# Second self attention of a decoder: scores as three products of rounded halves, and two slots for projection weights

## The chip, the cores and the metric

One core of a Trainium2 chip runs the whole program. The metric is device time in microseconds (us), the median of the runs, lower is better. The engines that matter here are TensorE (PE in the rows, its weight loads PEld), VectorE (DVE), ScalarE (ACT), GpSimd (POOL) and SyncE (SP), which issues the transfers.

## The reference, cut to what matters

The program is a decoder of two layers (self attention, cross attention, feed forward, each followed by a layer norm). The change lies in the second layer's self attention: 4 batches of 512 tokens, width 512, 16 query heads of 128, 4 key and value heads, rotary embedding, causal mask.

```python
xqkv = x @ Wqkv
xq = apply_rotary_emb(xq)                  # [b, 512, 16, 128]
xk = apply_rotary_emb(xk)                  # [b, 512, 4, 128]
xk = jnp.repeat(xk, g, axis=2)             # g = 4
xv = jnp.repeat(xv, g, axis=2)
scores = jnp.einsum('bqhd,bkhd->bhqk', xq, xk) * scale + causal_add[None, None]
probs = jax.nn.softmax(scores, axis=-1)
attn = jnp.einsum('bhqk,bkhd->bqhd', probs, xv).reshape(B, S, q_size)
x = _layernorm(x + attn @ Wo, axis=-1)
```

## The kernel before

`self_attention_1` handles one batch after another: three in a loop (`Fori`), the fourth written out behind it. In a batch, TensorE first does the pieces of `FIRST`: keys 0 and 1, a tile of values, key 2, a tile of values, key 3, query 0. Then it goes through `plan`, an order of 72 steps. Step 4h+j makes the scores of head h for the 128 query rows of tile j. A tile has only the keys that the causal mask leaves, so its scores are 128, 256, 384 or 512 columns wide. Ahead of the scores of every fourth step (j = 0) stands the projection of the NEXT head's query, `("query", h+1)`. Four steps after its scores a tile of probabilities is transposed ("turn", L109), and at step 4h+1 the values product of head h-2 follows (L1832). The products with `Wo` ("out", L1849) come in four rounds: 4 tiles of 8 heads at step 39, 4 tiles of 4 heads from step 58, 4 tiles of 2 heads from step 65, and 4 tiles of 2 heads at step 71.

Projections (L1785), value tiles (L1798) and the out products take their operands as two rounded halves, high and low (type `F32R`), and sum three products: high by high, high by low, low by high. Scores (L1820) and values products (L1832) are plain float32 matmuls; each shows in the trace as two records, that is "x2" for one score tile.

A projected query goes into one of two PSUM banks, `mm`. The other engines work in the order of their own programs, and each instruction waits for semaphores:

- VectorE applies the rotary embedding in `rotate`: three multiplications with the tables (L1922) from the bank, a drain, one addition (L1928) into `q_cols` or `k_cols`, which also frees the bank. For query h+1, which is projected in step 4h, it does so at its own step 4h+2 (`QUERY_LAG = 2`), ahead of that step's mask. In each step it adds the mask to the diagonal block (L1977), finds the row maximum (L1979) and takes the reciprocal of the sum of the step before (L1984). It also makes the low half of the attention output (L1942).
- ScalarE, in each step: the high half of the attention output where there is one (L1869), the copy of the transposed probabilities out of PSUM (L1877), the exponential of this step's scores (L1885), and the multiplication of the last step's probabilities by the reciprocal (L1891).
- GpSimd has only the end of the layer norm to do in a batch.
- SyncE loads the weights. `load_projection(p)` (L1714) brings the high and low halves of projection p (0 to 3 the keys, 4 to 19 the queries, 512 KB each) into slot p modulo `WEIGHT_SLOTS`; ahead of it SyncE waits until the projection that held the slot is done. At the start of the stage it issues key 0, the tables, key 1, the values weight (2 MB), then projections 2 and 3, then the halves of `Wo` (4 MB in three transfers, L1719), and only then does it wait for the first slot.

The lines that order TensorE at a head's first tile:

```python
elif kind == "scores":
    h, j = divmod(n, NT)
    if j == 0:
        pe.wait_ge(s.mm.free, b * MM + s.mm.size + mm_at["query", h] + 1)
    pe.wait_ge(s.sc.free, b * SC + NT + n + 1)
```

Of the kernel before, what the change touches and what calls it, by code (L numbers as in the profile page):

```python
# [27 lines left out]
P = 128  # L28
# [1597 lines left out]
def self_attention_1(nc, m, tables_in, packed):  # L1626
# [8 lines left out]
    TURN_LAG, VALUES_LAG, OUT_LAG = 4, 6, 8  # L1635
    QUERY_LAG = 2
    SLOTS = 5
    WEIGHT_SLOTS = 4
    PROJECTIONS = KV_HEADS1 + HEADS1


# [32 lines left out]
    with ExitStack() as ctx:  # L1674
# [2 lines left out]
        wo = sb("wo", [P, HALF_HEADS, 2, D], F32R)  # L1677
        tables, mask = sb("tables", [P, 2, S]), sb("mask", [P, P])
        x_high, x_low = sb("x_high", [P, KD, S], F32R), sb("x_low", [P, KD, S], F32R)
        k_cols, v_rows, q_cols = sb("k_cols", [P, KV_HEADS1, S]), sb("v_rows", [P, NT, KV_HEADS1 * HD1]), sb("q_cols", [P, 2, S])  # L1680
        turned_part = sb("turned_part", [P, S])
        neg_max, row_sum, inv_sum = sb("neg_max", [P, TILES]), sb("row_sum", [P, TILES]), sb("inv_sum", [P, TILES])
        probs = sb("probs", [P, SLOTS, S])
        x_rows = probs[:, 0:NT, :]
# [3 lines left out]
        s = Names()  # L1688
        s.x_loaded, s.max_ready, s.inv_ready, s.probs_ready, s.made = (sem(n) for n in ("x_loaded", "max_ready", "inv_ready", "probs_ready", "made"))
        s.var_ready, s.rstd_ready = sem("var_ready"), sem("rstd_ready")  # L1690
        s.x_high_ready, s.att_high_ready, s.shift_made = sem("x_high_ready"), sem("att_high_ready"), sem("shift_made")
        s.weights_in, s.wo_in = [sem(f"weights_in_{i}") for i in range(WEIGHT_SLOTS)], [sem(f"wo_in_{i}") for i in range(len(OUTS) - 1)]
        w_v, tables_loaded = sem("w_v"), sem("tables_loaded")
# [4 lines left out]
        def batches(engine, turn_x, batch):  # L1698

            turn_x(0)  # L1700
            with engine.Fori(0, B - 1) as b:
                batch(b, False)
            batch(B - 1, True)

        def bank_of(p):

# [53 lines left out]
        def _(pe):  # L1760
# [13 lines left out]
            def batch(b, last_one):  # L1774
# [33 lines left out]
                for step in plan:  # L1808
                    for kind, n in step:
                        if kind == "query":  # L1810
                            project(KV_HEADS1 + n)
                        elif kind == "v":
                            tile_values(n)
                        elif kind == "scores":
                            h, j = divmod(n, NT)
                            if j == 0:
                                pe.wait_ge(s.mm.free, b * MM + s.mm.size + mm_at["query", h] + 1)
                            pe.wait_ge(s.sc.free, b * SC + NT + n + 1)
                            t = (j + 1) * P
                            pe.matmul(sc[n % 4][:, 0:t], q_cols[:, h % 2, j * P:t], k_cols[:, h // GROUP, 0:t],  # L1820
                                      start=True, stop=True).then_inc(s.sc.full, 1)
                        elif kind == "turn":
                            pe.wait_ge(s.probs_ready, b * TILES + n + 1)
                            pe.wait_ge(s.ta.free, b * TA + n + 1)
                            turn_tile(pe, ta[n % 2], probs[:, n % SLOTS, :], m.ident[:], n % NT + 1).then_inc(s.ta.full, 1)
                        elif kind == "values":
                            g = mm_at[kind, n]
                            kv = n // GROUP
                            pe.wait_ge(s.ta.free, b * TA + s.ta.size + (n + 1) * NT)
                            pe.wait_ge(s.mm.free, b * MM + g + 1)  # L1830
                            for c in range(NT):
                                last = pe.matmul(mm[g % 2][:, c * P:], v_rows[:, c, kv * HD1:(kv + 1) * HD1],  # L1832
                                                 probs_t[:, n % 2, c, c * P:], start=c == 0, stop=c == NT - 1)
                            last.then_inc(s.mm.full, 1)
                        elif kind == "x" and not last_one:
                            turn_x(b + 1)
                        elif kind == "out":
                            o, j = divmod(n, NT)
                            first, end = OUTS[o]
                            if j == 0:  # L1840
                                for part in (range(3) if o == 0 else (o - 1,)):
                                    pe.wait_ge(s.wo_in[part], b * 32 + (16 if o == 0 else 32))
                            g = mm_at[kind, n]
# [12 lines left out]
        def _(act):  # L1856
# [4 lines left out]
                    act.copy(x_high[:, :, j * P:(j + 1) * P], blocks_of(sc[j], KD)).then_inc(s.x_high_ready, 1)  # L1861

            def batch(b, last_one):
                for now, step in enumerate(plan):
                    for kind, n in plan[now - 1] if now else ():
                        if kind == "values":
                            g = mm_at[kind, n]
                            act.wait_ge(s.mm.full, b * MM + g + 1)
                            act.copy(att_high[:, n % HALF_HEADS, :], mm[g % 2]).then_inc(s.att_high_ready, 1)  # L1869
# [33 lines left out]
        def _(dve):  # L1903
# [8 lines left out]
            def batch(b, last_one):  # L1912
# [1 line left out]
                dve.wait_ge(s.made, 2)  # L1914
                cos, sin = tables[:, 0, :], tables[:, 1, :]

                def rotate(to, g, scale):

                    dve.wait_ge(s.mm.full, b * MM + g + 1)
                    half = P // 2  # L1920
                    def times(to, rows, table):
                        dve.scalar_tensor_tensor(to, mm[g % 2][rows, :], scale, table, ALU.mult, ALU.mult)  # L1922

                    times(to, slice(0, P), cos)
                    times(turned_part[0:half, :], slice(half, P), sin[half:P, :])
                    times(turned_part[half:P, :], slice(0, half), sin[0:half, :])
                    dve.drain()
                    dve.tensor_tensor(to, to, turned_part[:], ALU.add).then_inc(s.mm.free, 1)  # L1928

                def deferred(kind, n):  # L1930
                    if kind == "x":
                        if not last_one:
                            low_x(b + 1)
                        return
                    g = mm_at[kind, n]
                    if kind == "query":
                        dve.drain()
                        rotate(q_cols[:, n % 2, :], g, 1.0)
                    elif kind == "values":
                        dve.wait_ge(s.mm.full, b * MM + g + 1)  # L1940
                        dve.wait_ge(s.att_high_ready, b * HEADS1 + n + 1)
                        dve.tensor_tensor(att_low[:, n % HALF_HEADS, :], mm[g % 2], att_high[:, n % HALF_HEADS, :].bitcast(F32),  # L1942
                                          ALU.subtract).then_inc(s.mm.free, 1)
                    elif kind == "v":
                        dve.wait_ge(s.mm.full, b * MM + g + 1)
                        dve.tensor_copy(v_rows[:, n, :], mm[g % 2]).then_inc(s.mm.free, 1)
                    else:
                        o, j = divmod(n, NT)
                        x = m.x_tok[:, b * NT + j, :]
                        dve.wait_ge(s.mm.full, b * MM + g + 1)  # L1950
                        dve.tensor_tensor(x, mm[g % 2], x, ALU.add).then_inc(s.mm.free, 1)
                        dve.drain()
                        if o == len(OUTS) - 1:
                            tile_statistics(dve, st, j, x)

                for kind, n in FIRST:
                    if kind == "key":
                        dve.drain()
                        rotate(k_cols[:, n, :], mm_at[kind, n], SCALE)
                    else:  # L1960
                        deferred(kind, n)
                def after(kind, n):
# [28 lines left out]

        @block.gpsimd
        def _(pool):
            pool.memset(mask[:], 0.0).then_inc(s.made, 1)
            pool.wait_ge(s.made, 1)
            pool.affine_select(out=mask[:], in_=mask[:], compare_op=ALU.is_ge, fill=MASK_NEG, base=0,
                               pattern=[[-1, P]], channel_multiplier=1).then_inc(s.made, 1)

            def batch(b, last_one):
                layernorm_rstd(pool, st, b, m, s)  # L2000
                pool.wait_ge(s.rstd_ready, b + 1)
                pool.tensor_tensor(shift[:], neg_mean[:], st.rstd[:], ALU.mult).then_inc(s.shift_made, 1)
# [965 lines left out]
```

## Time and profile before

| | |
|---|---|
| median of 3 runs | 2902.24 us (2897.63 to 2905.83) |
| profiled execution, span from first to last instruction | 2871.8 us |
| median less that span | 30.4 us |
| stage of the change | about 1130 to 1967 us of the span |
| TensorE busy, whole program | 2673.5 us (93%) |
| VectorE, ScalarE, GpSimd busy | 1806.2, 1420.3, 294.5 us |
| mean granted TensorE clock | 0.973 |

Of the profiled execution only the span is shown; the runs' times include what lies around it. Times in the rows are microseconds from the span's start. In a timeline, a row is one or several instructions of a kind in a row ("x2"), with the start of the first, the time from there to the end of the last, and in brackets how long the engine had been idle and what ended that. Instructions of one engine can overlap by about 0.1 us in the records, so distances are taken from start to start.

### The profile page before, as it was taken

Reading aid. Unit: us, or ns where it says so; the run is one execution under the profiler, and the core shown is the slowest. Engines: PE = TensorE matmul, PEld = TensorE weight load, DVE = VectorE, ACT = ScalarE, POOL = GpSimd, SP = SyncE. Lnnn points to the kernel's source line nnn. Section 1 sums busy time; section 2 is a strip of 40 time slices with the busy share of each in tenths; the row PEclk is TensorE's granted clock in tenths of the full one; section 3 lists DMA queues with packets and bytes.
Section 4 is the critical chain, followed back from the end, with each engine's and each line's share of the span. In section 5 each row is a group of like instructions: output and inputs, shape, how many; then the busy total and the mean of one; then the engine's idle time right before and its main releaser. Section 6 shows DMA issues by size and latency. Waiting matters only on the chain. (4 is left out here: it accounts for less than half of the span.)

```text
span 2871.8 us, 40570 instructions
## 1 busy us (share of the span) xinstructions
PE 2673.5 (93%) x12750; PEld 1685.2 (59%) x12750; DVE 1806.2 (63%) x3475; ACT 1420.3 (49%) x2978; POOL 294.5 (10%) x399
## 2 busy tenths in 40 slices
PE   8999997979999987999999999997999999997898
PEld 4555554444588863677777777775545455443444
DVE  5666674654543326756755756754777777775676
ACT  4454463322133322554553653743577676664665
POOL 1230003001711114000000000001110101000000
PEclk9999998989999999999999999998899999999999
DMA  3395105541687754323223223211000000001000
GB/s 140 86 123 143 58 15 184 186 141 54 200 277 234 248 184 148 115 103 109 73 106 110 68 104 124 66 67 59 5 6 6 5 2 5 2 2 71 26 23 30
DMA packets 114169, 266.30 MB, mean 93 GB/s; under 512 B 14464, under 2 KB 37008, under 8 KB 113200
## 3 DMA queue, kind: packets, MB, share of 16 engines
q1 hardware_dynamic: 97152, 211.16, 22.2%
q0 software_dynamic: 16816, 52.64, 7.8%
q8 instruction: 104, 1.70, 0.2%
q14 instruction: 97, 0.79, 0.1%
HBM read 208.97 MB, written 58.48 MB: 93 GB/s over the span
## 5 line engine op out<-in xcount | busy, mean ns | idle before, releaser
L2506 DVE TENSOR_REDUCE x_neg_max<-bank 128x1 f32<-128x512 f32 x512 | 327.1, 684 | 99.7 <-PE bank L2351 99.2
L2458 ACT ACTIVATE x_weights<-bank 128x512 f32<-128x512 f32 x512 | 279.1, 599 | 127.8 <-PE bank L2362 122.9
L1885 ACT ACTIVATE a_probs<-bank,a_neg_max 128x128 f32<-128x128 f32 (+3 forms) x256 | 136.1, 532 | 206.0 <-DVE a_neg_max L1979 202.0
L1785 PE MATMUL bank<-a_x_high,a_weights 128*128 128x512 f32 x640 | 218.3, 404 | 8.2 <-DMA a_weights<-split_qkv 2.3
L109 PEld LDWEIGHTS bank<-all_ident,a_probs 128*128 128x128 f32 x1200 | 151.5, 140 | 85.0 <-issue 47.0
L109 PE MATMUL bank<-all_ident,a_probs 128*128 128x128 f32 x1200 | 193.3, 273 | 3.0 <-ACT a_probs_t L1877 2.2
L1877 ACT COPY a_probs_t<-bank 128x128 f32<-128x128 f32 (+3 forms) x256 | 107.6, 420 | 144.2 <-PE bank L109 143.8
L1820 PE MATMUL bank<-a_k_cols,a_q_cols 128*128 128x128 f32 (+3 forms) x512 | 176.7, 434 | 0.4 <-DVE a_q_cols L1928 0.2
L1849 PE MATMUL bank<-a_wo,a_att_high 128*128 128x512 f32 x512 | 162.1, 398 | 3.9 <-DVE a_q_cols L1928 2.9
L1510 DVE TENSOR_TENSOR moe_acc<-bank,moe_acc 128x512 f32 x79 | 54.6, 692 | 171.1 <-PE bank L1176 170.5
L1165 PE MATMUL bank<-moe_gh_cols,moe_item 128*128 128x256 f32 x632 | 151.8, 383 | 3.0 <-DMA moe_item<-moe_items 2.7
L1176 PE MATMUL bank<-moe_item,moe_wide 128*128 128x256 f32 x632 | 149.4, 379 | 0.0
L1832 PE MATMUL bank<-a_probs_t,a_v_rows 128*128 128x512 f32 (+3 forms) x512 | 148.6, 433 | 0.0
L1264 ACT ACTIVATE moe_wide<-bank,moe_item 128x256 f32<-128x256 f32 x158 | 66.3, 471 | 161.6 <-PE bank L1165 129.1
L1785 PEld LDWEIGHTS bank<-a_x_high,a_weights 128*128 128x128 f32 x640 | 121.3, 189 | 39.6 <-issue 6.2
L1891 ACT ACTIVATE a_probs<-a_probs,a_inv_sum 128x128 f32<-128x128 f32 (+3 forms) x256 | 142.0, 555 | 2.7 <-DVE a_inv_sum L1984 2.7
L2351 PE MATMUL bank<-x_k_cols,x_q_cols 64*128 64x512 f32 x512 | 136.6, 498 | 3.5 <-DVE x_neg_max L2506 3.4
L1979 DVE TENSOR_REDUCE a_neg_max<-bank 128x1 f32<-128x128 f32 (+3 forms) x256 | 125.7, 491 | 18.8
L2384 PE MATMUL bank<-x_weights,x_v_rows 128*17 128x512 f32 x1024 | 135.7, 603 | 0.0
L1165 PEld LDWEIGHTS bank<-moe_gh_cols,moe_item 128*128 128x128 f32 x632 | 118.1, 191 | 22.9 <-DMA moe_item<-moe_items 7.4
L2362 PE MATMUL bank<-x_q_cols,x_k_cols 64*128 64x512 f32 x512 | 128.1, 419 | 3.2 <-ACT x_weights L2458 2.8
L1176 PEld LDWEIGHTS bank<-moe_item,moe_wide 128*128 128x128 f32 x632 | 119.9, 190 | 16.8 <-issue 0.3
(413 smaller groups left out, 5437.0 us busy)
## 6 DMA issues: line engine op xcount, KB each, us to landing
a_weights<-split_qkv SPq DMA_DIRECT2D x80, 512.0 KB, 3.6
moe_item<-moe_items SPq DMA_DIRECT2D x79, 257.0 KB, 3.8
moe_item<-moe_items SPq DMA_DIRECT2D x79, 256.0 KB, 3.7
a_wo<-split_out SPq DMA_DIRECT2D x8, 2048.0 KB, 7.8
a_wo<-split_out SPq DMA_DIRECT2D x16, 1024.0 KB, 9.9
split_qkv<-x_qkv_parts SPq DMA_DIRECT2D x12, 1024.0 KB, 5.1
moe_items<-in_L_ffn_e_w POOLq DMA_DIRECT2D x40, 256.0 KB
split_out<-a_turned SPq DMA_DIRECT2D x8, 1024.0 KB, 4.0
```

The source lines that it names most:

```text
L109: last = pe.transpose(bank[:, c * P:(c + 1) * P], rows[:, c * P:(c + 1) * P], ident)
L1165: last = pe.matmul(bank(("hidden", i))[:, c * TOKENS:(c + 1) * TOKENS], weight[:, k, c * P:(c + 1) * P], x_now[:, i % 2, k * TOKENS:(k + 1 ...
L1176: last = pe.matmul(bank(("item", i))[:, j * LATENT:(j + 1) * LATENT], hid[:, i % 2, c * TOKENS + j * P:c * TOKENS + (j + 1) * P], weight[: ...
L1785: last = pe.matmul(mm[g % 2], weight[:, k, :], x[:, k, :], start=n == 0, stop=n == 3 * KD - 1)
L1820: pe.matmul(sc[n % 4][:, 0:t], q_cols[:, h % 2, j * P:t], k_cols[:, h // GROUP, 0:t], start=True, stop=True).then_inc(s.sc.full, 1)
L1832: last = pe.matmul(mm[g % 2][:, c * P:], v_rows[:, c, kv * HD1:(kv + 1) * HD1], probs_t[:, n % 2, c, c * P:], start=c == 0, stop=c == NT - 1)
L1849: last = pe.matmul(mm[g % 2], att[:, at, j * P:(j + 1) * P], wo[:, at, part, :], start=h == first and att is att_high and part == 0, stop= ...
L1885: act.activation(probs[:, n % SLOTS, 0:t], sc[n % 4][:, 0:t], ACT.Exp, bias=neg_max[:, n:n + 1], accum_out=row_sum[:, n:n + 1]).then_inc(s ...
L1891: act.activation(probs[:, i % SLOTS, 0:t1], probs[:, i % SLOTS, 0:t1], ACT.Copy, scale=inv_sum[:, i:i + 1]).then_inc(s.probs_ready, 1)
L2351: pe.matmul(score_banks[slot % 3], q_cols[rows, u % 2, pair, j * P:(j + 1) * P], k_cols[rows, u % 2, pair, :], start=True, stop=True).then ...
L2458: act.activation(weights[:, chunk % 2, k, :], weight_banks[slot % 2], ACT.Exp).then_inc(s.weight.free, 1)
L2506: dve.tensor_reduce(neg_max[:, g % 2, j, h:h + 1], score_banks[slot % 3], AX.X, ALU.max, negate=True) \
```

## The change

- `rotate` no longer writes `q_cols` or `k_cols`. It writes a buffer `rotated` with two places (projection p in place p modulo 2). The bank is freed by the third multiplication instead of the addition. Ahead of it stands a new wait until GpSimd is done with the projection that had the place.
- ScalarE rounds `rotated` to the high half (`high_cols`): for the four keys and query 0 ahead of its step 0, for query h+1 at the very start of its step 4h+3, ahead of that step's copy, exponential and multiplication.
- GpSimd makes the low half, `rotated` less high, for all 20 projections of the batch.
- TensorE waits at a head's first tile for GpSimd's count instead of the bank, and makes each score tile from three `F32R` products instead of one plain float32 matmul.
- `WEIGHT_SLOTS` is 2 instead of 4, so SyncE's start brings only projections 0 and 1 ahead of `Wo`, and each later load waits for the projection two before it instead of four.

```diff
-    WEIGHT_SLOTS = 4
+    WEIGHT_SLOTS = 2
...
+        def parts_of(p):
+
+            if p < KV_HEADS1:
+                return k_high[:, p, :], k_low[:, p, :]
+            return q_high[:, (p - KV_HEADS1) % 2, :], q_low[:, (p - KV_HEADS1) % 2, :]
...
                             if j == 0:
-                                pe.wait_ge(s.mm.free, b * MM + s.mm.size + mm_at["query", h] + 1)
+                                pe.wait_ge(s.cols_split, b * PROJECTIONS + KV_HEADS1 + h + 3)
                             pe.wait_ge(s.sc.free, b * SC + NT + n + 1)
                             t = (j + 1) * P
-                            pe.matmul(sc[n % 4][:, 0:t], q_cols[:, h % 2, j * P:t], k_cols[:, h // GROUP, 0:t],
-                                      start=True, stop=True).then_inc(s.sc.full, 1)
+                            parts = ((q_high, k_high), (q_high, k_low), (q_low, k_high))
+                            for i, (q, k) in enumerate(parts):
+                                last = pe.matmul(sc[n % 4][:, 0:t], q[:, h % 2, j * P:t], k[:, h // GROUP, 0:t],
+                                                 start=i == 0, stop=i == len(parts) - 1)
+                            last.then_inc(s.sc.full, 1)
...
             def batch(b, last_one):
+                def high_cols(p):
+                    act.wait_ge(s.rotated, b * PROJECTIONS + p + 1)
+                    act.copy(parts_of(p)[0], rotated[:, p % 2, :]).then_inc(s.cols_high, 1)
+
+                for p in range(KV_HEADS1 + 1):
+                    high_cols(p)
                 for now, step in enumerate(plan):
+                    for kind, n in plan[now - QUERY_LAG - 1] if now > QUERY_LAG else ():
+                        if kind == "query":
+                            high_cols(KV_HEADS1 + n)
                     for kind, n in plan[now - 1] if now else ():
...
-                def rotate(to, g, scale):
-
+                def rotate(p, g, scale):
+
+                    to = rotated[:, p % 2, :]
                     dve.wait_ge(s.mm.full, b * MM + g + 1)
+                    dve.wait_ge(s.cols_split, b * PROJECTIONS + p + 1)
                     half = P // 2
...
-                    times(turned_part[half:P, :], slice(0, half), sin[0:half, :])
+                    times(turned_part[half:P, :], slice(0, half), sin[0:half, :]).then_inc(s.mm.free, 1)
                     dve.drain()
-                    dve.tensor_tensor(to, to, turned_part[:], ALU.add).then_inc(s.mm.free, 1)
+                    dve.tensor_tensor(to, to, turned_part[:], ALU.add).then_inc(s.rotated, 1)
...
         def _(pool):
+            pool.sem_inc(s.cols_split, 2)
...
             def batch(b, last_one):
+                for p in range(PROJECTIONS):
+                    high, low = parts_of(p)
+                    pool.wait_ge(s.cols_high, b * PROJECTIONS + p + 1)
+                    pool.tensor_tensor(low, rotated[:, p % 2, :], high.bitcast(F32), ALU.subtract).then_inc(s.cols_split, 1)
                 layernorm_rstd(pool, st, b, m, s)
```

## Rows read from the trace of the kernel before

**Rows 1.** The page: busy time of each engine over the whole span.
```profile
PE 2673.5 (93%) x12750; PEld 1685.2 (59%) x12750; DVE 1806.2 (63%) x3475; ACT 1420.3 (49%) x2978; POOL 294.5 (10%) x399
```

**Rows 2.** Windows: stretch, length, busy time of PE, PEld, DVE, ACT, POOL; granted clock; DMA.
```profile
1223.70:1231.80 8.10, 8.10 (x39) 5.90 (x38) 6.50 (x17) 6.16 (x19) 0.00 (x0) 1.00 0.17 65
1354.30:1358.50 4.20, 4.20 (x13) 3.29 (x14) 2.76 (x4) 0.11 (x1) 0.00 (x0) 0.66 0.00 0
```

**Rows 3.** Timeline of TensorE: the first score tile of heads 0, 1, 3, 9, 10, 14, 15; batch 1.
```profile
1164.11 0.92 PE L1820 MATMUL bank<-a_k_cols,a_q_cols 128*128 128x128 f32 x4 [0.21 <-DVE a_q_cols L1928]
...
1175.76 0.38 PE L1820 MATMUL bank<-a_k_cols,a_q_cols 128*128 128x128 f32 x2
...
1191.02 0.38 PE L1820 MATMUL bank<-a_k_cols,a_q_cols 128*128 128x128 f32 x2
...
1239.98 0.38 PE L1820 MATMUL bank<-a_k_cols,a_q_cols 128*128 128x128 f32 x2
...
1270.28 0.38 PE L1820 MATMUL bank<-a_k_cols,a_q_cols 128*128 128x128 f32 x2
...
1302.92 0.38 PE L1820 MATMUL bank<-a_k_cols,a_q_cols 128*128 128x128 f32 x2
...
1312.09 0.39 PE L1820 MATMUL bank<-a_k_cols,a_q_cols 128*128 128x128 f32 x2
...
1373.70 0.92 PE L1820 MATMUL bank<-a_k_cols,a_q_cols 128*128 128x128 f32 x4
```

**Rows 4.** Timeline of TensorE through one head (head 7 of batch 0).
```profile
1223.66 0.38 PE L1820 MATMUL bank<-a_k_cols,a_q_cols 128*128 128x128 f32 x2
1223.88 0.27 PE L109 MATMUL bank<-all_ident,a_probs 128*128 128x128 f32 x1
...
1227.78 1.02 PE L1820 MATMUL bank<-a_k_cols,a_q_cols 128*128 128x512 f32 x2
1228.64 0.60 PE L109 MATMUL bank<-all_ident,a_probs 128*128 128x128 f32 x4
...
1229.31 0.40 PE L1785 MATMUL bank<-a_x_low,a_weights 128*128 128x512 f32 x1
...
1230.00 0.39 PE L1785 MATMUL bank<-a_x_low,a_weights 128*128 128x512 f32 x1
```

**Rows 5.** Timeline of VectorE through the same head.
```profile
1224.08 0.30 DVE L1977 TENSOR_TENSOR bank<-bank,a_mask 128x128 f32<-128x128 f32 x1 [1.10 <-PE bank L1820]
...
1225.74 0.69 DVE L1922 SCALAR_TENSOR_TENSOR a_q_cols<-bank,a_tables 128x512 f32<-128x512 f32 x1 [0.17 <-issue]
```

**Rows 6.** Timeline of ScalarE in the same head: the first instruction of step 4h+3.
```profile
1230.44 0.58 ACT L1877 COPY a_probs_t<-bank 128x512 f32<-128x512 f32 x1
```

**Rows 7.** Timeline in the cross attention, which splits a tile into halves by the same two engines.
```profile
1990.82 1.04 ACT L2442 CAST x_split<-x_rot 128x1024 fp32r<-128x1024 f32 x1 [1.31 <-DVE x_rot L2549]
1991.95 1.27 POOL L2589 TENSOR_TENSOR x_split<-x_rot,x_split 128x512 fp32r<-128x512 f32 x1 [16.13 <-ACT x_split L2442]
...
1994.76 0.40 PEld L109 LDWEIGHTS bank<-x_ident_r,x_split 128*128 128x128 f32 x4 [0.83 <-ACT x_q_cols L2422]
```

**Rows 8.** Timeline of VectorE at the front of batch 1.
```profile
1363.88 0.69 DVE L1928 TENSOR_TENSOR a_k_cols<-a_k_cols,a_turned_part 128x512 f32<-128x512 f32 x1
...
1372.88 0.69 DVE L1928 TENSOR_TENSOR a_q_cols<-a_q_cols,a_turned_part 128x512 f32<-128x512 f32 x1
1374.22 0.30 DVE L1977 TENSOR_TENSOR bank<-bank,a_mask 128x128 f32<-128x128 f32 x1 [0.65 <-PE bank L1820]
```

**Rows 9.** Timeline of TensorE at the front of batch 0: key 2 and query 0.
```profile
1145.40 0.39 PE L1785 MATMUL bank<-a_x_high,a_weights 128*128 128x512 f32 x1
...
1156.53 0.50 PE L1785 MATMUL bank<-a_x_high,a_weights 128*128 128x512 f32 x1 [2.27 <-DMA a_weights<-split_qkv]
```

**Rows 10.** Transfers of projection weights, 1125 to 1200 us: time from issue to landing.
```profile
DMA to landing us min/median/max: 3.3/4.6/17.8
```

**Rows 11.** Transfers from 1129 to 1160 us: GB/s in 40 equal slices.
```profile
GB/s 0 0 122 301 383 394 333 412 418 418 423 423 418 428 386 391 418 412 381 386 418 412 412 412 423 407 423 412 418 412 412 407 391 418 418 412 412 291 58 16
```

More of the change, by code:

```diff
@@ L1679, in self_attention_1 @@
         x_high, x_low = sb("x_high", [P, KD, S], F32R), sb("x_low", [P, KD, S], F32R)
-        k_cols, v_rows, q_cols = sb("k_cols", [P, KV_HEADS1, S]), sb("v_rows", [P, NT, KV_HEADS1 * HD1]), sb("q_cols", [P, 2, S])
-        turned_part = sb("turned_part", [P, S])
+        k_high, k_low = sb("k_high", [P, KV_HEADS1, S], F32R), sb("k_low", [P, KV_HEADS1, S], F32R)
+        q_high, q_low = sb("q_high", [P, 2, S], F32R), sb("q_low", [P, 2, S], F32R)
+        v_rows = sb("v_rows", [P, NT, KV_HEADS1 * HD1])
+        rotated, turned_part = sb("rotated", [P, 2, S]), sb("turned_part", [P, S])
         neg_max, row_sum, inv_sum = sb("neg_max", [P, TILES]), sb("row_sum", [P, TILES]), sb("inv_sum", [P, TILES])
@@ L1690, in self_attention_1 @@
         s.var_ready, s.rstd_ready = sem("var_ready"), sem("rstd_ready")
+        s.rotated, s.cols_high, s.cols_split = sem("rotated"), sem("cols_high"), sem("cols_split")
         s.x_high_ready, s.att_high_ready, s.shift_made = sem("x_high_ready"), sem("att_high_ready"), sem("shift_made")
@@ L1915, in batch @@
                 cos, sin = tables[:, 0, :], tables[:, 1, :]
-                def rotate(to, g, scale):
+                def rotate(p, g, scale):
+                    to = rotated[:, p % 2, :]
                     dve.wait_ge(s.mm.full, b * MM + g + 1)
+                    dve.wait_ge(s.cols_split, b * PROJECTIONS + p + 1)
                     half = P // 2
                     def times(to, rows, table):
-                        dve.scalar_tensor_tensor(to, mm[g % 2][rows, :], scale, table, ALU.mult, ALU.mult)
+                        return dve.scalar_tensor_tensor(to, mm[g % 2][rows, :], scale, table, ALU.mult, ALU.mult)
                     times(to, slice(0, P), cos)
                     times(turned_part[0:half, :], slice(half, P), sin[half:P, :])
-                    times(turned_part[half:P, :], slice(0, half), sin[0:half, :])
+                    times(turned_part[half:P, :], slice(0, half), sin[0:half, :]).then_inc(s.mm.free, 1)
                     dve.drain()
-                    dve.tensor_tensor(to, to, turned_part[:], ALU.add).then_inc(s.mm.free, 1)
+                    dve.tensor_tensor(to, to, turned_part[:], ALU.add).then_inc(s.rotated, 1)
                 def deferred(kind, n):
@@ L1937, in deferred @@
                         dve.drain()
-                        rotate(q_cols[:, n % 2, :], g, 1.0)
+                        rotate(KV_HEADS1 + n, g, 1.0)
                     elif kind == "values":
@@ L1958, in batch @@
                         dve.drain()
-                        rotate(k_cols[:, n, :], mm_at[kind, n], SCALE)
+                        rotate(n, mm_at[kind, n], SCALE)
                     else:
```

## The prediction, written before the changed kernel was run

> **What bounds the kernel now.** I read the page first: TensorE is busy 2673.5 of 2871.8 us [rows 1]. That is an average over stages, so I looked at the stage of the change by windows of one head. In an undisturbed head TensorE is busy for the whole 8.10 us, while VectorE has 6.50 us and ScalarE 6.16 us of work, and GpSimd none [rows 2]. Then I took the distances between the heads' first score tiles in TensorE's timeline: heads 3 to 9 take 48.96 us, six times 8.16; heads 10 to 14 take 32.64, four times 8.16 [rows 3]. The other distances are 11.65 us from head 0 to 1, 15.26 over the two heads from 1 to 3, 30.30 from 9 to 10 (the round of out products of 8 heads) and 9.17 from 14 to 15. The four batches look alike to some hundredths. So mid-batch is bound by TensorE alone: what TensorE saves there comes back, as long as nothing that the change adds is slower than the head. Last I followed one head through the timelines of VectorE and ScalarE [rows 5, 6], since the change puts two more engines between a rotated query and its first score tile.
>
> **TensorE's work: less, by little.** A plain score tile of 512 columns takes 1228.64 - 1227.78 = 0.86 us, one of 128 takes 0.22 [rows 4]; both are 1.68 ns a column, so the 1280 columns of a head take 2.15 us. A rounded product of 512 columns takes (1230.00 - 1229.31) / 3 = 0.23 us [rows 4]. There is no rounded product narrower than 512 columns in the trace, except transposes. By columns, 384 take 0.17 and 256 take 0.12. For 128 columns I take 0.11, the pace of one record of a plain tile; rounded transposes of this width have four weight loads in 0.40 us [rows 7], so the pace may be a little better. Three products of each width are 3 x (0.11 + 0.12 + 0.17 + 0.23) = 1.89 us. Saved: 0.26 us a head, 17 us over 64 heads if all of it shows. The upper bound for a narrow product is the whole plain tile, 0.22 us: then the 128-column tile takes 0.66 instead of 0.33 us, and the saving is gone.
>
> The Trainium skill, in "FP8 and Floating Point Precision", TensorE Precision Notes, says that true FP32 takes four passes. Three passes for four would save a quarter of 2.15, 0.54 us a head. The wide tile's row gives 0.69 for 0.86, less than that, and the narrow ones are further off.
>
> **ScalarE's and GpSimd's work: hidden as work.** ScalarE gets one rounding a head. The cross attention's takes 1.04 us for 1024 columns out of SBUF [rows 7]; half of that is 0.52 and leaves the fixed part out, and ScalarE's copy of 512 columns out of PSUM takes 0.58 [rows 6]. I take 0.62, bounds 0.52 and 0.7. ScalarE is then at 6.8 us a head, GpSimd at 1.27 [rows 7]; neither is a bound by load.
>
> **The chain they form is not hidden.** This is the step that decides. Query h+1 is rotated at VectorE's step 4h+2, behind the mask, maximum and reciprocal of the first two tiles. ScalarE reaches `high_cols` at the start of its step 4h+3, thus behind the exponential of tile 2, whose mask VectorE does only after the rotation. So the new rounding starts where step 4h+3's copy starts now, at 1230.44 [rows 6]. Counted from the mask of the head's first tile, 1224.08 [rows 5], that is 6.36 us, and all in it hangs on that first tile: VectorE's first reciprocals (the rotation starts at 1225.74, without a wait for a bank), 2.8 us of rotation, mask and maximum of 384 columns, its exponential, one multiplication. Then:
>
> - from the mask of tile 0 to the rounding: 6.36
> - rounding: 0.62
> - ScalarE's end to GpSimd's start: 1991.95 - 1991.86 = 0.09, take 0.08 [rows 7]
> - GpSimd's subtraction: 1.27 to 1.28 [rows 7]
> - GpSimd's end to the mask of the next head's tile 0: where TensorE waits for the rotation's end now (1372.88 + 0.69 = 1373.57), the mask follows at 1374.22 [rows 8], 0.65 us. With three products for two records, one more start of 0.11: 0.75.
>
> The sum is 9.09 us from head to head. TensorE has 8.16 - 0.26 = 7.90 us of work in that time, so it will wait some 1.2 us a head, at the first tile, with its next projection already done. This wait holds up all that stands behind in TensorE's order: the turns, the values product, the other tiles. The products' saving lies inside the wait and is lost. The ten undisturbed heads gain 0.93 each: +9.3 us a batch.
>
> The other distances. Heads 1 to 3: two chains, 18.18 for 15.26, +2.9. Head 14 to 15: 9.09 for 9.17, -0.1. Heads 9 to 10: TensorE has 30 us of work, so the chain is hidden, -0.26; head 15, -0.3. Head 0 to 1: two value tiles stand in TensorE's order. TensorE saves 0.26, and the bank of query 1 is freed 0.7 us earlier by the third multiplication: -1.0. Together +10.5 a batch, 42 us for four.
>
> The Trainium skill, "GPSIMD Engine Reference", Engine selection, advises against GpSimd for elementwise work with two inputs, about twice as slow as VectorE. Its Instruction dispatch section puts the floor at about 2.5 cycles an element, an estimate of 1.07 us for 512; the row has 1.27, and by the page's figure the chain would be 0.2 shorter, some 10 us over the stage.
>
> **Fronts.** In batches 1 to 3 query 0's addition ends at 1373.57 and the mask comes at 1374.22 [rows 8]. The new chain behind the addition is 0.06 + 0.62 + 0.08 + 1.28 + 0.75 = 2.8 for 0.65, +2.1. Against it, keys free their banks 0.7 earlier at two places where TensorE waits for them (key 3 waits for the addition that starts at 1363.88 [rows 8]); I take 1.1 back, bounds 0 and 1.5. So +1.0 each, 3 us. Two slots are enough there: a load takes 3.3 to 4.6 us [rows 10], and between the projection that frees a slot and the one that needs it lie two others of 2.75, but for query 1, which waits 0.8 us inside the chain's wait.
>
> Batch 0 is different: keys 2 and 3 were loaded ahead of `Wo`. Now key 2's load is issued when key 0 is done and stands behind 4 MB of `Wo`. Today that place in the queue is held by query 0's load, issued 17.8 us before it lands [rows 10] at 1156.5 [rows 9]. With two loads of 512 KB fewer ahead, at some 415 GB/s [rows 11], key 2 lands 2.5 us earlier, at 1154.0. TensorE wants it at 1145.4 [rows 9]. From 1154: key 2, a value tile, key 3 and query 0 at 2.75 each, plus 1.8 for the lower clock after so long a pause (after a pause of 3.3 us the granted clock is 0.66 for 4.2 us [rows 2]), 1166.8. The rotation ends 3.3 later, 1170.1, the mask comes 2.8 behind it, 1172.9. Today it is at 1164.11 + 0.52 [rows 3]: +8 us. Bounds: 4, if transfers share and key 2 overtakes, and 10.
>
> **Sum.** 42 + 3 + 8 = +53 us on the profiled span of 2871.8: 2925. The median of the runs is 30.4 above that span, and nothing of the change lies outside, so 2955.
>
> **Rivals.**
> - *Narrow rounded products are slow* (chance 0.24). Nothing in the trace shows one. With 0.66 us for the first tile the chain grows by 0.3 at 13 heads of each batch: +16 us, 2971. TensorE's total doesn't decide, as it waits anyway.
> - *The chain is hidden and TensorE's saving shows* (0.08, the other side). It needs the chain to be under 7.90 us, 1.2 less than I count; at 8.16 it breaks even. Against it: 6.36 of the 9.09 are read as they stand, and GpSimd alone is 1.27. For it: GpSimd's records are rough. Then -17, -3 for the value tiles, +11 at the fronts: 2893. By the page on four passes it would be -35 for -17: 2875.
> - *The chain is half as bad* (0.12): ScalarE's and GpSimd's steps of 512 columns take 0.3 us less together, and batch 0 only 4 us more. 13 x 4 x 0.3 = 16 less, and 4 less: 2935.
> - *Nothing moves* (0.03), the chain just at the old 8.16 with batch 0's loss balanced: 2902.
> - The forecast itself: 0.53.
>
> **Chances.** A measurement tells from no change what is over 0.3%, 8.7 us. Slower: 0.53 + 0.24 + 0.12 = 0.89. Same 0.04, faster 0.07. The range reaches from under the half-bad chain to above slow narrow products with their bounds (a front cost of 10 us in batch 0, nothing won back at the others): 2928 to 2985.
>
> **What would show it.** Right: in mid-batch the first score tiles stand about 9.1 us apart, with TensorE idle 1.2 us ahead of them and GpSimd named as releaser; the subtraction takes 1.27 and ends just ahead of each; the 512-column tile takes 0.69. In batch 0 TensorE waits some 8 us for key 2's load. Wrong: a distance of 7.9 (the chain is hidden), or 9.4 with 128-column products of 0.2 us or more (the first rival). The forecast fails most easily in the 6.36: if the order of ScalarE's instructions lets the rounding start earlier, all ten heads change with it.

## The result, and the profile after

The changed kernel takes 2965.3 us (median of 4 runs, 2962.6 to 2967.0), the kernel before 2900.4 (4 runs, 2897.6 to 2905.8): the ratio is 1.0215, with a 95% interval of 1.0199 to 1.0230. The forecast was 2955, with a range of 2928 to 2985.

The page of the changed kernel, its busy times, and further down the group of its new score products (the last numbers are TensorE's idle time before them and who ended it):

```profile
PE 2678.8 (90%) x13006; PEld 1717.4 (58%) x13006; DVE 1807.3 (61%) x3475; ACT 1462.7 (49%) x3058; POOL 396.7 (13%) x479
...
L1831 PE MATMUL bank<-a_k_high,a_q_high 128*128 128x128 f32 (+3 forms) x256 | 99.4, 388 | 61.8 <-POOL a_q_low L2027 61.8
```

Against [rows 1], TensorE's busy time is about the same, its share has fallen from 93 to 90%, and 61.8 us of idle time now end with GpSimd's subtraction. I measured the stage from its first transposes of `x` to the first transposes of the cross attention: 844.5 us before (1130.35 to 1974.87), 909.6 after (1165.55 to 2075.17), so +65.1, and that is the whole difference between the medians.

TensorE's timeline of the changed kernel in batch 0: the waits at the front, then the first score tiles of heads 1, 2, 8, 9 and 10.

```profile
1188.83 0.79 PE L1794 MATMUL bank<-a_x_high,a_weights 128*128 128x512 f32 x1 [8.16 <-DMA a_weights<-split_qkv]
...
1203.61 0.47 PE L1794 MATMUL bank<-a_x_high,a_weights 128*128 128x512 f32 x1 [1.05 <-DMA a_weights<-split_qkv]
...
1208.10 0.32 PE L1831 MATMUL bank<-a_k_high,a_q_high 128*128 128x128 f32 x1 [1.48 <-POOL a_q_low L2027]
...
1219.04 0.22 PE L1831 MATMUL bank<-a_k_high,a_q_high 128*128 128x128 f32 x1
...
1228.08 0.32 PE L1831 MATMUL bank<-a_k_high,a_q_high 128*128 128x128 f32 x1 [3.01 <-POOL a_q_low L2027]
...
1283.62 0.32 PE L1831 MATMUL bank<-a_k_high,a_q_high 128*128 128x128 f32 x1 [0.97 <-POOL a_q_low L2027]
...
1293.12 0.32 PE L1831 MATMUL bank<-a_k_high,a_q_high 128*128 128x128 f32 x1 [1.32 <-POOL a_q_low L2027]
...
1323.69 0.22 PE L1831 MATMUL bank<-a_k_high,a_q_high 128*128 128x128 f32 x1
```

Where a steady head took 8.16 us [rows 3] it now takes 9.15 (1283.62 less 1274.47, below), and GpSimd is named ahead of its first tile. The rest of the chain, from one head's first mask to the next one's (all engines, head 6 of batch 0):

```profile
1265.91 0.30 DVE L2000 TENSOR_TENSOR bank<-bank,a_mask 128x128 f32<-128x128 f32 x1 [1.97 <-PE bank L1831]
...
1267.66 0.69 DVE L1945 SCALAR_TENSOR_TENSOR a_rotated<-bank,a_tables 128x512 f32<-128x512 f32 x1 [0.25 <-issue]
...
1269.85 0.69 DVE L1951 TENSOR_TENSOR a_rotated<-a_rotated,a_turned_part 128x512 f32<-128x512 f32 x1
...
1272.39 0.61 ACT L1878 CAST a_q_high<-a_rotated 128x512 fp32r<-128x512 f32 x1
...
1273.08 1.27 POOL L2027 TENSOR_TENSOR a_q_low<-a_rotated,a_q_high 128x512 fp32r<-128x512 f32 x1 [7.88 <-ACT a_q_high L1878]
...
1274.47 0.32 PE L1831 MATMUL bank<-a_k_high,a_q_high 128*128 128x128 f32 x1 [0.98 <-POOL a_q_low L2027]
...
1275.06 0.30 DVE L2000 TENSOR_TENSOR bank<-bank,a_mask 128x128 f32<-128x128 f32 x1 [1.98 <-PE bank L1831]
```

Read it as the forecast's sum. Mask to rounding 6.48, rounding to subtraction 0.69, subtraction 1.27, its end (1274.35) to the mask 0.71: together 9.15. The rotated query is complete at 1270.54, but ScalarE comes to it only at 1272.39, behind the exponential of tile 2 and a multiplication. Those 1.85 us are a matter of ScalarE's order alone. TensorE's own work in a head is 7.91 us (e1, below), so it loses 1.24 us a head, of which the row shows 0.98 as idle time.

Windows of the changed kernel: heads 1 and 2 and head 6 of batch 0, head 2 of batch 3 (length; busy time of PE, PEld, DVE, ACT, POOL; granted clock; DMA):

```profile
1219.04:1228.08 9.04, 6.03 (x36) 4.78 (x34) 5.91 (x16) 5.77 (x17) 1.27 (x1) 1.00 0.39 113
1228.08:1237.76 9.68, 9.68 (x43) 7.36 (x43) 6.70 (x17) 6.71 (x19) 1.30 (x1) 0.82 0.01 3
...
1265.91:1275.06 9.15, 8.17 (x44) 6.31 (x44) 6.51 (x17) 6.67 (x18) 1.27 (x1) 1.00 0.18 57
...
1894.80:1905.74 10.94, 10.94 (x42) 8.27 (x43) 6.70 (x17) 6.77 (x19) 1.29 (x1) 0.72 0.00 0
```

Head 6 is [rows 2] with a hole of 1 us in TensorE. Head 2 is another case: behind the 3.0 us wait at the end of head 1, TensorE is busy without a break and still takes 9.68 us in batch 0 and 10.94 in batch 3, at a mean granted clock of 0.82 and 0.72 (part of the stretch at 1.2 GHz instead of 2.4).

### The profile page after: what moved, and what is told of

Its sections match the earlier page's. It is cut to its first block and busy times, and to the rows that moved or that the text cites. A ratio compares the mean times of both kernels' runs of the same rounds, so it can differ in the third digit from the quotient of the medians.

```text
span 2963.0 us, 41485 instructions
## 1 busy us (share of the span) xinstructions
PE 2678.8 (90%) x13006; PEld 1717.4 (58%) x13006; DVE 1807.3 (61%) x3475; ACT 1462.7 (49%) x3058; POOL 396.7 (13%) x479
## 5 line engine op out<-in xcount | busy, mean ns | idle before, releaser
L2027 POOL TENSOR_TENSOR a_q_low<-a_rotated,a_q_high 128x512 fp32r<-128x512 f32 x64 | 81.5, 1274 | 577.7 <-ACT a_q_high L1878 577.7
L1831 PE MATMUL bank<-a_k_high,a_q_high 128*128 128x128 f32 (+3 forms) x256 | 99.4, 388 | 61.8 <-POOL a_q_low L2027 61.8
L2000 DVE TENSOR_TENSOR bank<-bank,a_mask 128x128 f32<-128x128 f32 x256 | 74.6, 291 | 131.4 <-PE bank L1831 129.2
L1794 PEld LDWEIGHTS bank<-a_x_high,a_weights 128*128 128x128 f32 x640 | 122.2, 191 | 45.4 <-issue 10.8
```

Of the source, the lines that this page charges most:

```text
L1794: last = pe.matmul(mm[g % 2], weight[:, k, :], x[:, k, :], start=n == 0, stop=n == 3 * KD - 1)
```

## The experiments

Every stage was measured as above; "front" is from the stage's first transposes to the first score tile of batch 0. Before: steady head 8.16, front 33.8, stage 844.5. Changed kernel: 9.15, 42.6, 909.6. The ratios are to the kernel before, run on the same chip.

| kernel | ratio (95%) | steady head | front | stage |
|---|---|---|---|---|
| e1 rounding earlier | 0.9983 (0.9971 to 0.9994) | 7.91 | 42.3 | 839.7 |
| e2 `Wo` behind keys 2, 3 | 1.0206 (1.0175 to 1.0237) | 9.15 | 38.9 | 907.2 |
| e3 subtraction twice | 1.0585 (1.0550 to 1.0620) | 10.55 | 44.4 | 1008.9 |
| e4 one plain product | 1.0217 (1.0182 to 1.0252) | 9.09 | 42.0 | 905.7 |
| e5 before, two slots | 1.0027 (1.0013 to 1.0040) | 8.16 | 40.5 | 851.7 |
| e6 e1, `Wo` behind six | 0.9958 (0.9938 to 0.9978) | 7.91 | 33.8 | 830.2 |
| e7 before, early bank | 0.9951 (0.9934 to 0.9968) | 8.16 | 32.0 | 829.6 |
| e8 e7, `Wo` behind six | 0.9937 (0.9915 to 0.9959) | 8.16 | 29.2 | 827.8 |
| e9 e1, one plain product | 1.0029 (1.0010 to 1.0047) | 8.16 | 43.2 | 851.0 |

**e1: the changed kernel with ScalarE's rounding one step earlier**, at step 4h+2, behind the copy and ahead of the exponential.

```diff
-                    for kind, n in plan[now - QUERY_LAG - 1] if now > QUERY_LAG else ():
-                        if kind == "query":
-                            high_cols(KV_HEADS1 + n)
                     for kind, n in plan[now - 1] if now else ():
...
                             act.copy(probs_t[:, h % 2, 0:j + 1, j * P:t], blocks_of(ta[n % 2], j + 1)).then_inc(s.ta.free, 1)
+                    for kind, n in plan[now - QUERY_LAG] if 0 <= now - QUERY_LAG < len(plan) else ():
+                        if kind == "query":
+                            high_cols(KV_HEADS1 + n)
                     for kind, n in step:
```

> ScalarE rounds query h+1 at its step 4h+2, behind that step's copy and ahead of its exponential, instead of at the start of step 4h+3; all else as in the changed kernel. If the wait for the split sets the head's length (the forecast's chain): the chain from mask to mask falls from 9.15 to 1.75 + 2.9 + 0.06 + 0.61 + 0.08 + 1.27 + 0.75 = 7.4 us, under TensorE's own work, which the changed kernel's trace puts at 8.0 us a head (9.15 less 0.98 of wait and 0.17 of drain). So first score tiles 8.0 us apart in mid-batch, no wait for GpSimd there, and some 17 us a batch less: about 2897. If something else makes the heads longer (slow narrow products, VectorE held up by GpSimd, the weight slots): the distances stay near 9.15 and the time at 2965.

Measured: 2899.7 us against 2905.1, ratio 0.9983. The timeline of e1, all engines, over one steady head, and its window:

```profile
1273.07 0.22 PE L1831 MATMUL bank<-a_k_high,a_q_high 128*128 128x128 f32 x1
...
1277.50 0.69 DVE L1951 TENSOR_TENSOR a_rotated<-a_rotated,a_turned_part 128x512 f32<-128x512 f32 x1
...
1278.11 0.29 DVE L2000 TENSOR_TENSOR bank<-bank,a_mask 128x128 f32<-128x128 f32 x1
...
1278.22 0.62 ACT L1878 CAST a_q_high<-a_rotated 128x512 fp32r<-128x512 f32 x1 [0.46 <-DVE a_rotated L1951]
...
1278.92 1.30 POOL L2027 TENSOR_TENSOR a_q_low<-a_rotated,a_q_high 128x512 fp32r<-128x512 f32 x1 [6.62 <-ACT a_q_high L1878]
...
1280.98 0.22 PE L1831 MATMUL bank<-a_k_high,a_q_high 128*128 128x128 f32 x1
```

```profile
1273.00:1280.91 7.91, 7.91 (x44) 6.39 (x43) 6.51 (x17) 6.75 (x19) 1.30 (x1) 1.00 0.24 67
```

ScalarE now rounds as soon as VectorE's addition has ended, the subtraction is done at 1280.22, and TensorE comes to the tile at 1280.98 with 0.76 us to spare. The same work by the same engines, in another order, takes 70 us less of the stage. What made the change slow is the place of the rounding in ScalarE's order, not the amount of work.

**e2: the changed kernel, with the loads of `Wo` issued behind those of keys 2 and 3.** The first batch does it like this, and the other batches load keys 2 and 3 of the next batch likewise ahead of its start:

```diff
-            for p in range(2, WEIGHT_SLOTS):
+            for p in range(WEIGHT_SLOTS, 2 * WEIGHT_SLOTS):
+                sp.wait_ge(s.mm.full, bank_of(p - WEIGHT_SLOTS) + 1)
                 load_projection(p)
             for o in range(3):
```

> SyncE loads keys 2 and 3 (each still behind the key that frees its slot) ahead of Wo at the start of the stage, two slots as in the changed kernel. If key 2's load is late in batch 0 because it stands behind 4 MB of Wo: TensorE's wait of 8.2 us for it goes, the first score tile of batch 0 comes about 34 us instead of 42.6 us behind the stage's first transposes, 9 us less, 2956; later batches and the head's 9.15 us don't move. If two slots cost time in every batch: 9 us are less than what they cost, and the fronts of batches 1 to 3 still show waits for weights.

Measured: ratio 1.0206; the front is 38.9 us instead of 42.6. TensorE's timeline of e2 shows the wait for key 2 gone, and another at query 0:

```profile
1199.34 0.79 PE L1798 MATMUL bank<-a_x_high,a_weights 128*128 128x512 f32 x1 [5.00 <-DMA a_weights<-split_qkv]
```

So the 8.16 us wait was for a load in the queue behind `Wo`; moving `Wo` two loads back pays 3.7 us of it and passes the rest on to the next load behind `Wo`. I had expected 9 us. Against the changed kernel's 1.0215 the ratio can't tell that from nothing; the front can.

**e3: the changed kernel, with GpSimd's subtraction done twice.**

```diff
+                    pool.tensor_tensor(low, rotated[:, p % 2, :], high.bitcast(F32), ALU.subtract)
+                    pool.drain()
                     pool.tensor_tensor(low, rotated[:, p % 2, :], high.bitcast(F32), ALU.subtract).then_inc(s.cols_split, 1)
```

> GpSimd makes each low half twice over (same result, a drain between). If its subtraction is a link of the chain: 1.3 to 1.4 us more at each of 13 chained distances of a batch and at each front, 56 x 1.35 = +75 us and some more, 3040 to 3050, first score tiles 10.5 us apart. If it is hidden, as its load of 1.27 us in a head of 9.15 would have it: no change, 2965.

Measured: 3070.8 us, ratio 1.0585, more than the 3040 to 3050 expected. GpSimd's timeline of e3, one head:

```profile
1284.12 1.27 POOL L2027 TENSOR_TENSOR a_q_low<-a_rotated,a_q_high 128x512 fp32r<-128x512 f32 x1 [7.87 <-ACT a_q_high L1878]
1285.53 1.26 POOL L2029 TENSOR_TENSOR a_q_low<-a_rotated,a_q_high 128x512 fp32r<-128x512 f32 x1
```

The second starts 1.41 us behind the first, and the steady head grows by 1.40, to 10.55: the subtraction lies in the chain in full. The stage grows by 99 us. 52 heads of 1.40 are 73 of them. The rest lies at the fronts, where eight of VectorE's 80 additions (0.69) are stretched, to as much as 1.64, and in single heads of 11 to 12 us. TensorE now waits 2.4 us in each steady head, and the head of 11.12 us from 1265.3 has a granted clock of 0.85, where the next one, of 10.55, has 1.00.

**e4 and e9: one plain product of the high halves instead of three rounded ones**, in the changed kernel (e4) and in e1 (e9). The two products with low halves are left out; ScalarE's and GpSimd's work stays.

```diff
-                            parts = ((q_high, k_high), (q_high, k_low), (q_low, k_high))
-                            for i, (q, k) in enumerate(parts):
-                                last = pe.matmul(sc[n % 4][:, 0:t], q[:, h % 2, j * P:t], k[:, h // GROUP, 0:t],
-                                                 start=i == 0, stop=i == len(parts) - 1)
+                            last = pe.matmul(sc[n % 4][:, 0:t], q_high[:, h % 2, j * P:t].bitcast(F32), k_high[:, h // GROUP, 0:t].bitcast(F32),
+                                             start=True, stop=True)
```

> Scores are one plain float32 product of the high halves (the two products with low halves are left out); split, waits and slots as in the changed kernel. If TensorE waits for the split anyway: its work rises by about 0.16 us a head, which disappears in its wait, and the chain loses one start of 0.11 us: 2958 to 2962. If TensorE's work on scores decides (or if narrow rounded products are what made the change slow): a move of at least 10 us, up by 0.16 x 64 = 10 if the three products save time, down by 15 or more if they cost it.

> The early rounding of e1 with one plain product of the high halves in place of the three rounded products; the two products that the low halves enter are left out. Theory: in e1 the chain is hidden and TensorE sets the head at 7.91 us, 0.25 below before's 8.16, because three rounded products cost 1.89 us where one plain product costs 2.15. With the plain product back and GpSimd's and ScalarE's work kept, the quiet heads should stand 8.16 apart, the stage should be some 0.25 x 64 = 16 us longer than e1's 839.7 (about 856), and the time about 2916. Rival: something other than TensorE sets e1's head (VectorE, ScalarE or the rounding chain); then the distance stays at 7.91 and the time at 2900.

Measured: e4 1.0217, e9 1.0029. TensorE's timeline, first of e4, then of e9, two heads in a row each:

```profile
1280.56 0.48 PE L1829 MATMUL bank<-a_k_high,a_q_high 128*128 128x128 f32 x2 [0.55 <-POOL a_q_low L2025]
...
1289.65 0.48 PE L1829 MATMUL bank<-a_k_high,a_q_high 128*128 128x128 f32 x2 [0.64 <-POOL a_q_low L2025]
```

```profile
1243.99 0.38 PE L1829 MATMUL bank<-a_k_high,a_q_high 128*128 128x128 f32 x2
...
1252.15 0.38 PE L1829 MATMUL bank<-a_k_high,a_q_high 128*128 128x128 f32 x2
```

In e4 the head is 9.09 for 9.15 (its first tile has two starts instead of three): 0.25 us more of TensorE's work a head comes out of the wait, and the time doesn't move. In e9, where the chain is hidden, the same edit gives 8.16 for 7.91 and a stage 11.2 us longer: ten steady heads by four batches by 0.25 are 10. The fronts, and the tiles behind a wait, don't show it, so I had expected too much with 16. The three rounded products save 0.25 us a head, and only where TensorE sets the pace.

**e5: the kernel before with `WEIGHT_SLOTS = 2`.**

> The kernel before with WEIGHT_SLOTS = 2 and nothing else of the change. If two slots cost only where Wo stands ahead of a load: batch 0's first score tile comes some 6 us later behind the stage's first transposes (33.8 before, 42.6 with the whole change, of which about 2 are the split of query 0), the other fronts at most 1 us for query 1's load, mid-batch stays at 8.16: about +6 to +9 us, ratio 1.002 to 1.003. If two slots starve mid-batch: distances above 8.16 there.

Measured: 2913.1 us, ratio 1.0027. The front is 6.8 us longer and the stage 7.2. TensorE waits 8.42 us for key 2's load, and the steady heads stay as they were: two slots cost batch 0's front, nothing in the steady heads.

**e6: e1 with the loads of `Wo` behind those of the first six projections.** The first batch issues them like this, and the others load projections 2 to 5 of the next batch likewise ahead of its start:

```diff
+            for p in range(WEIGHT_SLOTS, KV_HEADS1 + 2):
+                sp.wait_ge(s.mm.full, bank_of(p - WEIGHT_SLOTS) + 1)
+                load_projection(p)
             for o in range(3):
```

> The changed kernel with ScalarE's rounding at step 4h+2 (as the first experiment) and SyncE's Wo loads behind those of keys 2 and 3 and queries 0 and 1. The second experiment moved the wait from key 2 to query 0 (5.0 us, landed behind Wo); with no projection load behind Wo the first score tile of batch 0 should come some 34 to 35 us behind the first transposes instead of 42.3: 8 us less than the first experiment, about 2891, ratio to before near 0.9955. If transfers of the loads themselves are the limit, the gain is 4 us or less.

Measured: 2892.6 us, ratio 0.9958. Front 33.8, 8.5 less than e1's; stage 830.2. So with two slots and the split batch 0's front is back at the 33.8 us of the kernel before.

**e7 and e8: the kernel before with the bank freed early**, that is by the third multiplication instead of the addition; the scores wait for the addition by a count of its own. e8 also has `Wo` behind six loads, as e6.

```diff
-                                pe.wait_ge(s.mm.free, b * MM + s.mm.size + mm_at["query", h] + 1)
+                                pe.wait_ge(s.rotated, b * PROJECTIONS + KV_HEADS1 + h + 1)
...
-                    times(turned_part[half:P, :], slice(0, half), sin[0:half, :])
+                    times(turned_part[half:P, :], slice(0, half), sin[0:half, :]).then_inc(s.mm.free, 1)
                     dve.drain()
-                    dve.tensor_tensor(to, to, turned_part[:], ALU.add).then_inc(s.mm.free, 1)
+                    dve.tensor_tensor(to, to, turned_part[:], ALU.add).then_inc(s.rotated, 1)
```

> The kernel before with one part alone: the third multiplication frees the PSUM bank and the scores wait for the addition by a semaphore of their own. TensorE's waits for the rotation's end at the fronts, at head 0 and at head 14 get 0.7 us shorter each: distance 0 to 1 10.9 instead of 11.65, 14 to 15 8.4 instead of 9.17, fronts some 1.1 us shorter, mid-batch 8.16 as before. 10 us less in all, ratio 0.9965. Rival: the waits are taken up by the next one behind, and nothing moves.

> As the experiment before this one, and SyncE's Wo loads behind those of queries 0 and 1 (four slots, plain scores). Batch 0 loses its wait of 2.3 us for query 0's weights and 1.8 us of lower clock: 4 us less than without, 14 us less than before, ratio 0.995. It says whether the split is worth having at all: the first kernel of this set with the split against this one without.

Measured: e7 2891.8 us, ratio 0.9951; e8 2889.2, ratio 0.9937. Steady heads stay at 8.16; heads 0 to 1 take 10.89 for 11.65, 14 to 15 take 8.38 for 9.17, and the stage loses 14.9 us, where I had expected 10. So the part of the change that helps most has nothing to do with the split; the three products, the other part that saves time, show only where the chain is hidden (11 us between e1 and e9). e8 is the best kernel measured, though its interval overlaps e6's and e7's. e6 has 0.25 us less in each steady head, and gives it back at the fronts (33.8 for 29.2 in batch 0) and in head 1 to 2 (7.24 for 6.02), where the split's chain shows. So no run shows the split to be faster than the early bank without it.

**e10: the kernel before, once more**, to see what the 30.4 us between its first profile and its median were.

> The kernel before, unchanged, profiled once more. Theory: the first profile's span of 2871.8 us lay 30 us under its kernel's runs because that one execution was shorter ahead of the self attention stage (which began at 1130 us there and at 1165 to 1181 in every other profile). A second profile should then show the stage beginning at 1165 to 1180, lasting 844.6 within 1 us, with a span near 2900, some 2 us under the run. Rival: the kernel before really reaches the stage earlier than the others do; then it begins near 1130 again and the span is about 2872.

Measured: 2875.6 us, the one run that is profiled, span 2873.8, and 13 timed runs on that chip have a median of 2876.2. The stage starts at 1143.1 and lasts 843.8. The stage is as long as the theory said; its start fits neither, and the span is the rival's. A run's time lies only 1.8 us above its own span. On this chip the kernel's median is 24 to 29 us less than the 2900.4 to 2905.1 measured on the others, and the stage starts at 1143.1, against 1164.8 to 1181.1 in the profiles of the changed kernel and of e1 to e8. So chips differ, and mostly in what lies ahead of the stage (e9, on the same chip, starts it at 1149.7). That the first profile (start 1130.35) came from such a chip fits, but the chip it was taken on isn't known.

## Why the prediction was right, step by step

- **The chain of 9.09 us** measured 9.15; the rows of before that gave it [rows 5 to 8] stand against the chain above. Shown by three runs: doubling one link adds it in full (e3), taking 1.85 us of waiting out of it hides it (e1), and more work for TensorE doesn't move it (e4). The links: 6.48 for 6.36, 0.69 for 0.70, 1.27 for 1.28, 0.71 for 0.75. Of the 0.12, 0.09 stands ahead of the rotation ([0.25 <-issue] for 0.17 in [rows 5]), where the new wait is; in the batch written out behind the loop it is 0.16 for 0.09 before, and the head takes 8.99. So the new wait goes with 0.07 to 0.08 us in either place; that it causes them was not tried. The other two rivals fall with the distance: a hidden chain wanted 7.9, a chain half as bad 8.8.
- **TensorE's saving of 0.26 us a head, lost in the wait:** 0.25, lost in the changed kernel and seen in e1 (7.91, 0.25 under [rows 3]). TensorE's timeline of the changed kernel in head 6, the products of tiles 2, 3 and, a head later, 0:

```profile
1268.75 0.34 PE L1831 MATMUL bank<-a_k_low,a_q_high 128*128 128x384 f32 x1
1268.93 0.34 PE L1831 MATMUL bank<-a_k_high,a_q_low 128*128 128x384 f32 x1
...
1269.66 0.40 PE L1831 MATMUL bank<-a_k_low,a_q_high 128*128 128x512 f32 x1
1269.90 0.39 PE L1831 MATMUL bank<-a_k_high,a_q_low 128*128 128x512 f32 x1
...
1274.63 0.27 PE L1831 MATMUL bank<-a_k_low,a_q_high 128*128 128x128 f32 x1
1274.75 0.28 PE L1831 MATMUL bank<-a_k_high,a_q_low 128*128 128x128 f32 x1
```

  From start to start a rounded product takes 0.12 us at 128 columns, 0.18 at 384 and 0.24 at 512, where I had taken 0.11, 0.17 and 0.23. The rival of slow narrow products, 0.22 at 128, falls. By an estimate from the four passes that "FP8 and Floating Point Precision" of the Trainium skill, TensorE Precision Notes, gives for true FP32, three passes for four would save 0.54 a head; the runs show less than half of that.
- **Batch 0's front, +8:** +8.8. TensorE's wait for key 2's load behind `Wo` is 8.16 us, as forecast (some 8). The two slots alone make +6.8 (e5, without any split); the other 2.0 come with the rest of the change; the forecast had 2.1 for the split of query 0.
- **Fronts of the other batches with head 15, +0.7 together:** +0.9, -0.2 and +0.8, from head 15 to the next batch's head 0.
- **Heads 0 to 1, -1.0:** -0.7.
- **Heads 1 to 3, +2.9:** +3.5 in batch 0, +4.7 in batch 3 (from its 15.45), mis-sized. I put two chains there. The wait of 3.0 us at the end of head 1 is followed by a lower granted clock, and head 2 is then set by TensorE at that clock, not by the chain. In e4, where that wait is 2.79 in batch 0 and the clock stays at 1.00, head 2 takes the chain's 9.09. The prediction had priced such a fall at batch 0's front from [rows 2] and not here.
- **Heads 9 to 10, -0.26, and 14 to 15, -0.1:** +0.3 and +0.6, mis-sized. At both VectorE makes the low half of the attention output (0.68) between the rotation and tile 2's mask, which I left out. At head 9 TensorE's out products wait 0.54 us for it, where they waited for nothing before: counted from the head's first score tile the low half is done 0.27 us later (5.81 for 5.54), and TensorE, with less work on scores, comes to them sooner. In e1, where no head is late, the wait is 0.61. At head 14 the low half lies in the chain. VectorE's and ScalarE's timelines of the changed kernel at head 14, whose first mask is at 1360.77:

```profile
1364.71 0.69 DVE L1951 TENSOR_TENSOR a_rotated<-a_rotated,a_turned_part 128x512 f32<-128x512 f32 x1
...
1365.32 0.68 DVE L1965 TENSOR_TENSOR a_att_low<-bank,a_att_high 128x512 fp32r<-128x512 f32 x1
...
1365.92 0.29 DVE L2000 TENSOR_TENSOR bank<-bank,a_mask 128x128 f32<-128x128 f32 x1
...
1367.84 0.61 ACT L1878 CAST a_q_high<-a_rotated 128x512 fp32r<-128x512 f32 x1
```

  From mask to rounding it is 7.07 there, 0.59 more than in head 6.
- **Head 8 to 9** takes 9.50 in the three batches of the loop; the rotation starts 2.10 us behind the mask instead of 1.75, without a wait that the trace names. The same 0.35 us stand at this head in e1, e3, e4 and e9, and in the batch behind the loop at heads 1, 6 and 11 instead, so they go with a place in VectorE's program. The cause is left open; it is 1 us in the loop and less than that behind it.
- **The sum:** +53 forecast, +65 measured. From head 0 to head 15 a batch adds 13.4 to 13.9 us instead of 10.8. In batch 0 these 3.0 us more are 1.0 in the ten steady heads (most of it the chain's 0.06 a head and head 8), 0.3 at head 0, 0.5 in heads 1 and 2, 0.5 at head 9 and 0.7 at head 14. The fronts and heads 15 together make +10, as forecast. So the mechanism held, and every term inside a batch was somewhat low.
- **The offset of 30.4 us** was misread. I took it for time around the span, which is 1.8 us (e10); the rest is most likely a difference between chips. It did no harm to the sum: the forecast stands on the median of 2902.24, and the kernel before had 2900.4 beside the changed kernel.

## What to carry to other kernels

When work is handed to a second and third engine, look first at where it is put in their orders: the same rounding cost 2% at one place and nothing two instructions earlier. Count the chain between two visits of the pacing engine from row to row, with every instruction that stands ahead of a link in its engine's order, also those that come only in some heads; what the pacing engine saves is worth nothing until that chain is shorter than its work. A change with several parts should be priced in parts: here the early release of the bank alone is worth 0.5%, which the rest of the change buried.

## What the runs showed of the hardware

**VectorE's addition and GpSimd's subtraction collide.** The addition of two operands in SBUF takes 691 to 695 ns in 77 of its 80 instances in the changed kernel; the other three, keys at the fronts of batches 1 to 3, take 799, 1452 and 1797. VectorE and GpSimd at the front of batch 2, timeline of all engines:

```profile
1638.58 1.29 POOL L2027 TENSOR_TENSOR a_k_low<-a_rotated,a_k_high 128x512 fp32r<-128x512 f32 x1 [7.05 <-ACT a_k_high L1878]
1638.62 1.80 DVE L1951 TENSOR_TENSOR a_rotated<-a_rotated,a_turned_part 128x512 f32<-128x512 f32 x1
```

GpSimd started 40 ns earlier, and the addition ends 0.55 us after GpSimd does, as if it had waited and then run; so do the other two (0.55 and 0.54), which start 1.03 and 0.39 us behind GpSimd. In the other order it is GpSimd that is held up: in e9 an addition from 1592.92 takes its 0.69, and the subtraction that starts 0.09 us behind it takes 1.76 instead of 1.3. "SBUF — State Buffer" of the Trainium skill, Who interferes with whom, says that a VectorE instruction with two inputs in SBUF contends with a GpSimd instruction that reads SBUF, that the ports they share are an exclusive lock, and that the order of issue decides who is blocked; the rows agree. It is rare here, since in a steady head the two lie 2.5 us apart. The price is 0.1 to 1.1 us each time.

**A pause of 3 us is followed by a lower granted clock**, at a different price each time: the windows above have the same pause of 3.0 to 3.2 us and the same work behind it, at 0.82 in one batch and 0.72 in another, 1.26 us apart. In e4 the pause in batch 0 is 2.79 us, and the head behind it has 1.00.
